# A gated cross attention layer on one core: the attention stage rewritten with the values stationary and P normalised before its product

## The reference, cut to what matters

```python
x = layer_norm(x, g_norm)
q = x @ Wq
k, v = jnp.split(context @ Wkv, 2, axis=-1)
# heads; the null key and value go in front, so that each row has 129 keys
k = jnp.concatenate([nk, k], axis=2)
v = jnp.concatenate([nv, v], axis=2)
sim = jnp.einsum('bhid,bhjd->bhij', q * sqrt_scale, k * sqrt_scale)
sim = jnp.where(full_mask[:, None, None, :], sim, max_neg)
attn = jax.nn.softmax(sim, axis=-1)
out = jnp.einsum('bhij,bhjd->bhid', attn, v)
return layer_norm(out.reshape(b, -1, INNER) @ Wout, g_out)
```

## Time and profile before

| | |
|---|---|
| device time, median of 3 (all three) | 437.84 us (436.25, 437.84, 441.38) |
| profiled execution, span | 440.6 us |
| TensorE matmul busy, of the span | 367.1 us (83%) |
| TensorE weight load busy | 292.4 us (66%) |
| VectorE busy | 283.7 us (64%) |
| ScalarE busy | 232.7 us (53%) |
| GpSimd busy | 94.1 us (21%) |
| mean granted TensorE clock | 0.932 of full |
| DMA | 15.36 MB, mean 35 GB/s |

### The profile page before, as it was taken

One profiled execution on the slowest core, in us unless ns is written; L12 is line 12 of the kernel. 1 busy time (PEld: TensorE's weight loads), 2 busy tenths in 40 slices (PEclk: granted clock), 3 DMA queues, 4 the chain that ended last, 5 costly groups with the idle time before them and its releaser, 6 DMA issues.

```text
span 440.6 us, 9524 instructions
## 1 busy us (share of the span) xinstructions
PE 367.1 (83%) x2667; PEld 292.4 (66%) x2674; DVE 283.7 (64%) x892; ACT 232.7 (53%) x434; POOL 94.1 (21%) x248
## 2 busy tenths in 40 slices
PE   1899897998995779999999999999999999714432
PEld 1487475685663658888888888888888888612122
DVE  1777468547574546658667676686676867357964
ACT  1536956647675445554555555555555555307560
POOL 3322143223231121111211212122120211110012
PEclk9999999879997799999999999999999999967855
DMA  7900000000000201110101101011010110000003
GB/s 195 237 4 0 18 3 0 18 0 0 0 0 12 84 24 36 39 49 25 48 31 41 48 24 48 24 48 48 24 48 24 48 49 3 0 1 0 0 0 95
DMA packets 21139, 15.36 MB, mean 35 GB/s; under 512 B 4288, under 2 KB 20672, under 8 KB 21120
## 3 DMA queue, kind: packets, MB, share of 16 engines
q1 hardware_dynamic: 20400, 14.93, 11.3%
q10 hardware_dynamic: 720, 0.20, 0.3%
HBM read 5.69 MB, written 1.05 MB: 15 GB/s over the span
## 4 chain that ended last, share of the span: by engine, by line
PE 53%; DVE 19%; issue 13%; ACT 5%; POOL 4%; DMA 2%; DVEq 1%; SPq 1%; ACTq 0%; POOLq 0%
PE psum L1156 12%; PE psum L861 10%; PE psum L965 5%; PE psum L865 4%; PE psum L1180 4%; POOL rstd L514 3%; PE psum L866 3%; PE psum L867 3%; DVE work L1575 3%; PE psum L995 2%; DMA KT<-in_L_xattn_Wkv 2%; DVE st L1591 2%; PE psum L1052 1%; PE psum L1217 1%; DVE work L1666 1%
## 5 line engine op out<-in xcount | busy, mean ns | idle before, releaser
L861 PE MATMUL psum<-ident,work 128*128 128x128 f32 (+1 forms) x544 | 91.1, 285 | 15.5 <-DVE work L1648 5.8
L861 PEld LDWEIGHTS psum<-ident,work 128*128 128x128 f32 (+1 forms) x544 | 67.1, 154 | 24.2 <-DVE work L1648 7.7
L1156 PE MATMUL psum<-V,work 128*128 (+1 forms) x512 | 70.5, 281 | 9.2 <-DVE work L1575 4.7
L1156 PEld LDWEIGHTS psum<-V,work 128*128 128x128 f32 x512 | 61.9, 191 | 20.1 <-issue 12.5
L1528 DVE TENSOR_REDUCE mx<-psum 128x4 f32<-128x512 f32 x64 | 43.9, 686 | 36.5 <-PE psum L965 36.2
L801 ACT ACTIVATE work<-psum 128x256 f32<-128x256 f32 x64 | 24.5, 384 | 65.5 <-PE psum L861 65.5
L865 PE MATMUL psum<-split 128*128 128x256 f32 (+2 forms) x128 | 54.3, 424 | 0.2
L810 ACT ACTIVATE work<-psum 128x512 f32<-128x512 f32 x64 | 38.2, 597 | 28.7 <-PE psum L861 28.0
L965 PE MATMUL psum<-work 64*128 64x128 f32 x512 | 45.8, 297 | 0.7 <-ACT work L681 0.7
L593 POOL TENSOR_TENSOR work<-null_logit,mn 128x4 f32<-128x4 f32 x64 | 13.0, 203 | 151.1 <-DVE mn L1557 146.4
L866 PE MATMUL psum<-split 128*128 128x256 f32 (+2 forms) x128 | 45.2, 353 | 0.0
(11 more groups left out here) (174 smaller groups left out, 568.8 us busy)
## 6 DMA issues: line engine op xcount, KB each, us to landing
work<-KT SPq DMA_DIRECT2D x32, 256.0 KB, 2.5
out_x<-X SPq DMA_DIRECT2D x4, 256.0 KB, 2.3
KT<-in_L_xattn_Wkv SPq DMA_DIRECT2D x2, 384.0 KB, 6.7
X<-in_x SPq DMA_DIRECT2D x1, 768.0 KB, 6.9
work<-in_ctx SPq DMA_DIRECT2D x3, 192.0 KB, 2.5
work<-in_L_xattn_Wq SPq DMA_DIRECT2D x1, 512.0 KB, 7.4
KT<-in_L_xattn_Wout SPq DMA_DIRECT2D x1, 512.0 KB, 4.9
work<-in_L_xattn_Wout SPq DMA_DIRECT2D x1, 512.0 KB, 4.4
```

What stands on the lines that cost most here:

```text
L861: return pe.transpose(dst, src, ident[0:m, 0:m])
L1156: ins = pe.matmul(bank[5][:, j * VW:(j + 1) * VW], PTs[m % 2][:, j * S:(j + 1) * S], vb.rearrange("p o e -> p (o e)"), start=True, stop=True)
```

## The change

The attention stage is written out for all 64 units, without a loop, in steps n. Units are taken apart over steps: step n has the scores, the maximum and the exponential of unit n, the normalisation on GpSimd of unit n-1, the transposes of P and the value product of unit n-3 (`T_LAG`), the output projection of unit n-4 (`WO_LAG`).

- The null key is written as a 129th key into `KT` after the stage before, so the score product streams 129 columns and gives the null logit too. The product L1133 and the copies L782 and L785 go; `xT` is written at once. The logit scale is folded into `gn_col`.
- The maximum, negated, is the exponent's bias: four exponentials of 129 elements straight from PSUM, each with its own bias column and an accumulated sum, which goes to PSUM. The subtraction on VectorE and the in-place exponential of 516 elements go.
- The sum is corrected for masked keys (`masked`), inverted on VectorE, and GpSimd multiplies all 512 elements of P by it, and the null weights.
- P^T is copied out of PSUM by VectorE, no longer by ScalarE.
- In the value product V (64 columns) is stationary and P^T (128 columns) streams; heads alternate between output partitions 0 to 63 and 64 to 127. The result is already transposed: the two transposes, the division and the bank that they used go.
- Keys are read from `KT` in place; the key DMAs go. q comes in one chunk per step in place of two chunks in every second unit, and is copied out chunk by chunk.

The core of the diff:

```diff
-        V = sb("V", [P, B, NH, VW])
+        KT = sb("KT", [P, NCH, B * K1])
+        KTb = KT[:, :, :].rearrange("p c (b t) -> p c b t", b=B)
+        V = sb("V", [P, B, NH, DH])
         xT = sb("xT", [P, B * S])
-        null_logit = sb("null_logit", [P, B, NH])
...
+        T_LAG, WO_LAG = 3, 4
+        PNT_AT, NULL_AT, Y_AT, STATS_AT, X3_AT, XN4_AT = 9, 10, 12, 13, 15, 16
+        LAST = UPT * (NPAIR - 1) + XN4_AT + 1
...
+        def q_chunk(n):
+            t, c = (n + UPT - 2) // UPT, (n - 2) % UPT
+            return (t, c) if 1 <= t < NPAIR else None
...
-                sp.dma_start(kTs[:, slot:slot + 2, :],
-                             KT[:, 2 * hg:2 * hg + 2, bass.ds(turn * (2 * S), 2 * S)]).then_inc(k_copied[hg].sem, 16)
...
+            def fill_null_keys():
+                pool.wait_ge(kv_out.sem, kv_out.at(0, NG))
+                ones_of = nk_col[:, 0:1].rearrange("p (c o) -> p c o", c=1).to_broadcast([P, NCH, B])
+                pool.tensor_copy(KTb[:, :, :, S:K1].rearrange("p c b o -> p c (b o)"),
+                                 ones_of).then_inc(null_keys.sem, 1)
...
-                    pool.tensor_tensor(Sx[k % 4][:, :, S], nl, mn[k % 2][:, :], ALU.subtract).then_inc(null_sub.sem, 1)
...
+            def normalise(n):
+                b, hg = unit(n)
+                sx_ = Sx[n % 4]
+                pool.wait_ge(rden_done.sem, rden_done.at(n + 1))
...
+                pool.tensor_tensor(pnr[t % 2][:, b % 2, HPU * hg:HPU * hg + HPU], sx_[:, :, S], rden[n % 2][:, :],
+                                   ALU.mult).then_inc(pnr_done.sem, 1)
+                pool.tensor_tensor(sx_[:, :, 0:S], sx_[:, :, 0:S], bcast(rden[n % 2][:, :], S),
+                                   ALU.mult).then_inc(p_ready.sem, 1)
...
-                    act.activation(xTs, bank[3], ACT.Identity, scale=gn_col[:, 0:1]).then_inc(xTs_ready.sem, 1)
+                    act.activation(xT[:, bass.ds(f * T, T)], bank[3], ACT.Identity,
+                                   scale=gn_col[:, 0:1]).then_inc(xT_ready.sem, 1)
...
-                    act.activation(oTs[m % 2], bank[6][:, 0:2 * S], ACT.Copy).then_inc(ot_out.sem, 1)
...
-                    act.activation(PTs[m % 2], bank[4], ACT.Copy).then_inc(pt_out.sem, 1)
-                if not tail:
-                    act.wait_ge(sim_sub.sem, sim_sub.at(k + 1, turn))
-                    act.wait_ge(null_sub.sem, null_sub.at(k + 1, turn))
-                    act.activation(Sx[k % 4], Sx[k % 4], ACT.Exp, scale=ATT_SCALE).then_inc(exp_done.sem, 1)
...
+            def o_evac(m):
+                act.wait_ge(ot_done.sem, ot_done.at(m + 1))
+                if m >= 2:
+                    act.wait_ge(wo_done.sem, wo_done.at(m - 1))
+                act.activation(oTs[m % 2], bank[5][:, 0:2 * S], ACT.Copy).then_inc(ot_out.sem, 1)
...
+            def q_chunk_evac(t, c):
+                act.wait_ge(q_done.sem, q_done.at(q_count(t, c)))
+                act.wait_ge(sim_done.sem, sim_done.at(UPT * (t - 1) + 2 * (c // 2) + 2))
+                act.activation(qT[:, c, :], bank[6][:, 0:2 * S], ACT.Copy).then_inc(q_out.sem, 1)
+            def exponents(n):
+                act.wait_ge(max_done.sem, max_done.at(n + 1))
+                if n >= 4:
+                    act.wait_ge(pt_done.sem, pt_done.at(n - 3))
+                    act.wait_ge(pnr_done.sem, pnr_done.at(n - 3))
+                for j in range(HPU):
+                    here = 2 * (n % 2) + j % 2
+                    ins = act.activation(Sx[n % 4][:, j, :], psum[:, here, (j // 2) * K1:(j // 2 + 1) * K1], ACT.Exp,
+                                         bias=nmx[n % 2][:, j:j + 1],
+                                         accum_out=psum[:, 2 * (n % 2), 2 * K1 + j:2 * K1 + j + 1])
+                ins.then_inc(exp_done.sem, 1)
+            for n in range(LAST + 1):
+                t = pair_at(n, Y_AT)
+                if t is not None:
+                    y_evac(t)
+                if live(n - WO_LAG):
+                    o_evac(n - WO_LAG)
+                t = pair_at(n, NULL_AT)
+                if t is not None:
+                    pn_evac(t)
+                if q_chunk(n):
+                    q_chunk_evac(*q_chunk(n))
+                if live(n):
+                    exponents(n)
...
+            def scores(n):
+                b, hg = unit(n)
+                pe.wait_ge(q_out.sem, q_out.at(q_count(n // UPT, 2 * hg + 1)))
+                if n == 0:
+                    pe.wait_ge(null_keys.sem, null_keys.at(1))
+                if n >= 2:
+                    pe.wait_ge(den_done.sem, den_done.at(n - 1))
                 for j in range(HPU):
                     rows = slice(DH * (j % 2), DH * (j % 2) + DH)
-                    tk = slice(b * S, (b + 1) * S)
-                    ins = pe.matmul(bank[2 * (k % 2) + j % 2][:, (j // 2) * S:(j // 2 + 1) * S],
-                                    qT[rows, 2 * hg + j // 2, tk], kTs[rows, 2 * (hg % 2) + j // 2, tk],
-                                    start=True, stop=True)
+                    ins = pe.matmul(bank[2 * (n % 2) + j % 2][:, (j // 2) * K1:(j // 2 + 1) * K1],
+                                    qT[rows, 2 * hg + j // 2, (b % 2) * S:(b % 2 + 1) * S],
+                                    KTb[rows, 2 * hg + j // 2, b, :], start=True, stop=True)
                 ins.then_inc(sim_done.sem, 1)
...
-                        vb = V[:, bass.ds(turn * 2 + (m % 2) + (-2 if k < 2 else 0), 1), HPU * (m // 2) + j, :]
-                        ins = pe.matmul(bank[5][:, j * VW:(j + 1) * VW], PTs[m % 2][:, j * S:(j + 1) * S],
-                                        vb.rearrange("p o e -> p (o e)"), start=True, stop=True)
-                    ins.then_inc(pv_done.sem, 1)
...
-                    for j in range(2):
-                        ins = transpose(bank[6][:, j * S:(j + 1) * S], on[m % 2][:, j * S:(j + 1) * S])
-                    ins.then_inc(ot_done.sem, 1)
...
+            def p_transposes(m):
+                pe.wait_ge(p_ready.sem, p_ready.at(m + 1))
+                if m >= 1:
+                    pe.wait_ge(pt_out.sem, pt_out.at(m))
+                for j in range(HPU):
+                    ins = transpose(bank[4][:, j * S:(j + 1) * S], Sx[m % 4][:, j, 0:S])
+                ins.then_inc(pt_done.sem, 1)
+            def values(m):
+                b, hg = unit(m)
+                pe.wait_ge(pt_out.sem, pt_out.at(m + 1))
+                if m >= 1:
+                    pe.wait_ge(ot_out.sem, ot_out.at(m))
+                for j in range(HPU):
+                    rows = slice(DH * (j % 2), DH * (j % 2) + DH)
+                    ins = pe.matmul(bank[5][rows, (j // 2) * S:(j // 2 + 1) * S], V[:, b, HPU * hg + j, :],
+                                    PTs[m % 2][:, j * S:(j + 1) * S], start=True, stop=True)
+                ins.then_inc(ot_done.sem, 1)
...
+            def out_proj(m):
+                b, hg = unit(m)
+                t, k = divmod(m, UPT)
+                pe.wait_ge(ot_out.sem, ot_out.at(m + 1))
...
+                for j in range(2):
+                    ins = pe.matmul(bank[7][:, (b % 2) * D:(b % 2 + 1) * D], oTs[m % 2][:, j * S:(j + 1) * S],
+                                    wo[:, 2 * hg + j, :], start=(k == 0 and j == 0), stop=(k >= UPT - 2 and j == 1),
+                                    skip_group_check=True)
+                ins.then_inc(wo_done.sem, 1)
...
+            for n in range(LAST + 1):
+                if live(n - T_LAG):
+                    p_transposes(n - T_LAG)
+                if live(n) and n > 0:
+                    scores(n)
+                if q_chunk(n):
+                    t, c = q_chunk(n)
+                    pe.wait_ge(xs_ready.sem, xs_ready.at(t + 1))
+                    pe.wait_ge(q_out.sem, q_out.at(q_count(t, c) - 1))
+                    q_proj(t, c, bank[6][:, 0:2 * S]).then_inc(q_done.sem, 1)
+                if live(n - WO_LAG):
+                    out_proj(n - WO_LAG)
...
+                    values(n - T_LAG)
...
-                    dve.wait_ge(sim_done.sem, sim_done.at(k + 1, turn))
-                    dve.tensor_reduce(mx[:, :].rearrange("p (c a) -> p c a", a=2), sim, AX_X,
-                                      ALU.max).then_inc(max_done.sem, 1)
...
-                    dve.wait_ge(pv_done.sem, pv_done.at(k - 1, turn))
-                    dve.tensor_tensor(sm[:, :], o[:, :, DH], Sx[m % 4][:, :, S], ALU.add).then_inc(sum_done.sem, 1)
...
-                    dve.tensor_tensor(Sx[k % 4][:, :, 0:S].rearrange("p (c a) t -> p c a t", a=2), sim,
-                                      mn[k % 2][:, :].rearrange("p (c a o) -> p c a o", a=2,
-                                                                o=1).to_broadcast([P, 2, 2, S]),
-                                      ALU.subtract).then_inc(sim_sub.sem, 1)
...
-                    dve.tensor_tensor(on[m % 2].rearrange("p (h e) -> p h e", h=HPU), o[:, :, 0:DH],
```

(29 more changed lines are left out.)

506 lines of the change are left out of this document (182 added, 324 removed).

## The result

| | before | after |
|---|---|---|
| device time, median | 439.6 us (436.3 to 444.3, 4 executions) | 401.9 us (399.9 to 405.7, 4 executions) |
| ratio, 95% interval | | 0.915 (0.909 to 0.920) |
| profiled execution, span | 440.6 us | 397.8 us |
| first scores to fourth | 12.1 us | 9.7 us |
| fourth scores to last, 60 units | 206.2 us, 3.44 each | 173.6 us, 2.89 each |

The kernel is 37.7 us faster; I had forecast 21.7 and a range from 403 up, and the time lies just under it. Later executions of the same two programs gave 402.3 and 439.5 (0.918, 0.913 to 0.924).

The account below looks back on a forecast made before the run. TensorE's stream was taken to bound the kernel. The attention steps gave -16.2 us, block 0 -1.8, the stage's start -1.7 and its end -2: -21.7, so 416 us from 437.84, with a range of 403 to 433.

Parts of the forecast that it names:

- TensorE's stream bounds: Attention stage: TensorE's own issue sets the pace, 3.2 of 3.44 us per unit; other engines add 0.24 of waits.
- Its sum, 3.0 a step: TensorE's work per attention step after the change, 3.0 us, 0.2 under before, with the value product at 0.65 plus 0.20 entry.
- The rival of 3.35: Value product: column halves don't overlap, so TensorE needs 3.35 us a step, 3.45 with waits; 432 us, chance 0.16.
- Waits, two thirds of those of before, 0.17 a step: Attention steps: two thirds of the 0.24 us of waits per unit remain, making 3.17 us a step and -16.2 us.
- Writing the stage out costs nothing: Attention loop: writing it out changes nothing, since its first turn, already written out, is no faster than the loop.
- The ring, 3.96 + E for two steps: Projection, ScalarE's result copy and exponentials wait on each other in a circle; with exponentials E at 1.9, 2.95 us a step.
- The late maxima: VectorE: normalisation after the sums makes the next maximum 0.2 to 0.4 us late in three of eight steps.
- ScalarE 2.6, VectorE under 2, GpSimd 1.8: Work of each engine per attention unit after the change, in us; before it was 1.85, 2.37 and 0.69.
- GpSimd's product is hidden by the lag: Normalisation of P, 128 x 512, 1.26 us: wanted two steps later, so hidden as long as GpSimd fits in a step.
- The slow rival: GpSimd binds if its 128 x 512 product takes over 3.1 us; at 3.3, 3.8 a step and 454 us; chance 0.07.
- Block 0 -1.8, start -1.7, end -2: Savings in us outside the steady steps: null product's path in block 0, earlier exponentials at the stage's start, shorter drain.

Follow-up runs that it names:

- The version written out: The kernel before with its loop over the six middle pairs written out and nothing else changed: 436.8 us, 0.994 of before, 3.36 us a unit.

## Why the prediction fell short, step by step

- *TensorE's stream bounds.* Right, and more than I thought: in the steps of the changed kernel nothing else does.
- *Its sum, 3.0 a step.* It was 2.92 in a turn (2.81 and 0.11 for the null weights) and 2.89 over all, since the last turn has no q. The value product was mis-sized: 0.58 for 0.65. I had it rightly that the entry costs 0.20, but not that a record costs 0.107 as before, so that only an overlap of the halves could help. A record of 64 loaded columns takes 0.053, and taking the halves in another order changes nothing. The rival of 3.35 rested on the same error. The P transposes with the entry of the scores were 0.59 for 0.64. Together 0.1 a step, 6 us.
- *Waits, two thirds of those of before, 0.17 a step.* This is the step that failed most: there are none in the steps of a turn, 10 us. I had scaled the 0.24 of the kernel before as if it were one thing that goes on. The version written out shows three parts: the loop, 0.08; the wait for ScalarE's copy of P^T ahead of the value product, 0.09; and 0.07 of the null weights' step (5.06 against 3.62, 0.17 a unit over the stage, of which only 0.1 was in my sum). The change writes the loop out. It puts scores, q and projection between the P transposes and the value product, and the copy is there in time, also when ScalarE makes it (steps of 2.81 with it back there). And it brings the null weights down to 0.11.
- *Writing the stage out costs nothing.* Wrong: it gives 4.8 us of the 32.6. The comparison with the first turn misled me, since that one starts with an empty pipeline; its last four steps, 2.79, 3.61, 2.79 and 3.62, were already shorter than the loop's 2.79, 3.70, 3.10 and 3.69.
- *The ring, 3.96 + E for two steps.* Its form held to about 0.1 when ScalarE was loaded. E was 1.2 to the start of the result copy and 1.4 to the end of the last write-out, not 1.9, since a sum's write-out hides behind the next exponential; so 2.6 to 2.7 a step, under TensorE's 2.81 (with 1.9 it is 2.93, not the 2.95 that I wrote). The late maxima exist, 12 waits of up to 0.3 in 110 us, but the 0.5 of slack takes them.
- *ScalarE 2.6, VectorE under 2, GpSimd 1.8.* Measured 2.07, 2.17, 1.56. The two rows of VectorE's normalisations, 349 and 344 ns before, take 513 and 589 on the whole page beside GpSimd's product; that is 0.1 a unit, and the rest of what VectorE has over my figure I have not traced. GpSimd's product took 1.06 where I had 1.18 to 1.26.
- *GpSimd's product is hidden by the lag.* Right, and this is what the third step of lag is for: without it, and with VectorE's order as it is, the step would have been 3.71 and the change a loss of 4%. I did not see that the sum stands behind the maximum on VectorE. The slow rival had a mechanism much nearer than its threshold of 3.1 us.
- *Block 0 -1.8, start -1.7, end -2.* Start -2.4 (2.1 shown by the removal of the null logits' product alone). End -0.4: result copies and P^T copies come late in the drain, 3.6 us of waits in all. What block 0 gained can't be told from nothing: without its null product the kernel before had its first scores no earlier.

A turn of 27.95 us thus became one of 23.37, 0.57 a unit: loop 0.11, null weights 0.07, the wait for the P^T copy in the q steps and q itself 0.06, transposes of the result 0.22, value product 0.25, P transposes 0.05, less the entry of 0.20; 0.56 of it by these rows.

The sum: -32.6 in the stage, -2.4 at its start, -0.4 at its end, about -2 ahead of it: 37.4 for the 37.7 of the medians. The last term no run shows; it is the difference of two means whose executions lie up to 11 us apart, and that it closes the sum is partly luck.

## What to carry to other kernels

Before one scales the waits of a kernel into a forecast, one lists the intervals between equal events: a mean of 3.36 was 2.79, 3.62 and one 5.06, and 0.08 more was the loop. Of the three causes of its waits two went with the change and the third shrank. A wait behind another operation on an in-order engine can close a circle of one step; a step of lag breaks it, and it is worth its longer drain many times over (0.9 a step here against one step once), though putting the awaited operation first gave 0.6 of it without a longer lag. Products on half the array cost a charge where they meet full-array work, so they belong side by side.

## What the runs showed of the hardware

- The write-out of an exponential's sum has rows of 199 ns on ScalarE, but pairs follow each other every 0.30 us; without it the time does not change.
- A value product of eight records takes, to the start of the next group, 0.89 with 128 columns loaded and 128 streamed, 0.58 with 64 and 128, 0.56 with 32 and 128, 0.38 with 64 and 64.
- Two of VectorE's operations of 128 x 128 on SBUF took 0.54 and 0.57 in 110 us of the changed kernel's stage, and 1.17 and 1.14 when GpSimd had two large products a step, while its operations on PSUM kept their 0.69. Where VectorE's operation came first, GpSimd's product took 1.15 for 1.04.
- Programs with the same block 0 reached their first scores up to 11 us apart in single executions.
